# A routed three-way MLP on one core: the first group's rows in two gathers, its first layer by halves of tokens, and GpSimd's set-up moved around the ordering

## The chip, the core and the metric

The kernel runs on one core of one Trainium2 chip. The metric is the device time of one launch in microseconds, the median of three runs; the kernel before takes 102.68 us (101.89 to 102.86).

## What is computed

`x` is 64 sequences of 64 tokens with 256 features, float32. Each sequence has a condition 0, 1 or 2 that picks one of three small networks ("routes"); the result is added to `x` and layer-normalised.

```python
out_nr = gelu(x @ w1_nr + b1_nr) @ w2_nr + b2_nr                       # condition 0, 256 -> 256 -> 256
out_tsr = gelu(x @ w1_tsr + b1_tsr) @ w2_tsr + b2_tsr                  # condition 1
h = gelu(x @ w1_sr + b1_sr)                                            # condition 2, 256 -> 512
out_sr = gelu(h @ w2_sr + b2_sr) @ w3_sr + b3_sr
out = where(c == 0, out_nr, where(c == 1, out_tsr, where(c == 2, out_sr, 0)))
y = x + out
return (y - mean(y)) * rsqrt(var(y) + 1e-5) * gamma + beta
```

## The kernel before

**Ordering.** The kernel sorts the 64 sequences by route on the chip, so that groups of eight sequences (512 tokens) share one route. GpSimd writes constants (iota, memset, affine_select; L377 to L414) while the conditions are fetched. VectorE (DVE) turns the conditions into one-hot rows `own` (L666), TensorE (PE) counts them (L950, L951), and a chain of small VectorE instructions (L674 to L703) ends in `in_slot` and `row_at`. PE multiplies these (L953) into the row number that each of the 128 partitions has to fetch for each of ten groups, and VectorE converts them to integers, `load_idx` (L711). Each sequence is 16 rows of four tokens (4 KB each), so that eight sequences fill 128 partitions. GpSimd then issues indirect gathers `xs[g] <- x` (L421), the first three at once (`EARLY = 3`).

**Classes and places.** VectorE goes on to the table of the groups' classes (`cls_tab`, L716 to L732), copies the bias columns (L734), makes the low part of the first layer's weights (`w_low(0)`, L742), and builds `at_place` and `half_row_at` (L872 to L887), which PE multiplies into the places for the stores (L1142, L1143) and the rows of a half-size last group (L1146).

**Precision.** Every float32 product is three products of rounded parts. For a tensor `t`, ScalarE (ACT) copies the rounded high part `t_hi` and VectorE subtracts it to get `t_lo`; PE accumulates `w_lo*x_hi + w_hi*x_hi + w_hi*x_lo`. One 128-wide block of the first layer is thus six matmuls (two tiles of the 256 features, `kt`), of 512 columns (tokens) each.

**Steps.** PE transposes a group's rows into the PSUM pair `ps_x` (L962, eight 128x128 transposes), ACT copies `x_hi`, VectorE subtracts `x_lo`, and `layer1` (L979 to L991) runs. For the long route, `long_first` runs four blocks m = 0 to 3 into `ps_a0, ps_a1, ps_b, ps_a0`, ACT applies GELU twice (L563 the rounded part, L564 in place) and VectorE subtracts (`low`, L758). `long_second` is the second layer, `last_layer` (L1024, products L1045) the last. `last_layer` of group g-1 runs in step g. Then VectorE adds x and takes the statistics, GpSimd takes the root and multiplies by gamma and adds beta, and scatters (L480). In this run groups 0 and 1 are long.

**The head of the program.** PE's order is written by hand: ordering matmuls, the bias transpose (L956), ten matmuls on ones that only keep PE busy (`WARM`, L1136), the transposes of group 0 (each half of the features, `kt`, signalled apart), the places, and step 0. In step 0 the transposes of group 1 (`next_x`) stand between block 0 and block 1; ACT's `x_high(1)` and VectorE's `x_low(1)` stand behind their parts of block 0. SP's queue issues the long route's weights, waits for GpSimd's two memsets (`zeroed`, L337), issues the last-layer biases, gamma and beta, waits for group 0's rows (`x_loaded[0]`, L345), and issues the other routes' weights and the broadcast biases. GpSimd's memsets of the unused route's last weights (L428) stand ahead of the first gather. `consts` reaching `CONSTS` (17) says that all GpSimd constants are there; `ORDER_CONSTS` (10) that those of the ordering are.

## Time and profile before

| | |
|---|---|
| median of three runs | 102.68 us (101.89 to 102.86) |
| the profiled execution, its device time | 102.77 us |
| its span, first to last instruction | 101.1 us |
| PE matmul busy | 83.8 us (83%), 502 matmuls |
| PE weight load busy | 73.1 us (72%) |
| VectorE busy | 76.8 us (76%) |
| ScalarE busy | 66.6 us (66%) |
| GpSimd busy | 64.0 us (63%) |
| DMA | 13.01 MB, mean 129 GB/s |

Time that lies outside the span is 102.77 - 101.1 = 1.67 us. Names are PE (TensorE), PEld (its weight loads), DVE (VectorE), ACT (ScalarE), POOL (GpSimd), SP (the queue that issues most direct DMAs). "L962" is a line of the kernel. A matmul's duration includes the time to drain, so the pace of a row of matmuls is read from their starts, not from their durations.

### The profile page before, as it was taken

The page shows a single profiled execution, that of the slowest core. Times are in us where ns is not written, and L with a number is a line of the kernel's source. Part 1 is how long each engine was busy: PE and PEld are TensorE (multiplying, and loading weights), DVE is VectorE, ACT ScalarE, POOL GpSimd, SP SyncE. Part 2 cuts the span into 40 slices and gives each one's busy share as a digit, 9 for nine tenths or more (in the row PEclk, how much of TensorE's full clock was granted, in tenths as well). Part 3 has the DMA queues.
Part 4 walks back from the last instruction along what each step waited for, and adds up shares of the span by engine and source line. Part 5 has one row for each costly group of instructions (what it writes and reads, how often), then busy time and mean ns, then how long its engine had stood idle before and what let it go on. Part 6 is the DMA issues. An engine that isn't in the chain of part 4 may idle for free.

```text
span 101.1 us, 1747 instructions
## 1 busy us (share of the span) xinstructions
PE 83.8 (83%) x502; PEld 73.1 (72%) x502; DVE 76.8 (76%) x209; ACT 66.6 (66%) x108; POOL 64.0 (63%) x81
## 2 busy tenths in 40 slices
PE   0239999999999999999999999999999999960000
PEld 0137588887886988879989899898988999950000
DVE  5578966849775504985799999899999999899900
ACT  0667046999599503599999899998998990800000
POOL 7918605005977760040567898998889989899900
PEclk9999999999999999999999999999999999999755
DMA  0892899810028999300000220402205005051570
GB/s 0 261 358 47 284 336 321 207 17 0 0 47 311 281 366 409 152 0 6 0 0 6 89 122 6 183 5 96 118 0 208 6 0 214 0 182 39 208 242 20
DMA packets 5782, 13.01 MB, mean 129 GB/s; under 512 B 656, under 2 KB 3104, under 8 KB 5760
## 3 DMA queue, kind: packets, MB, share of 16 engines
q0 software_dynamic: 2672, 9.57, 25.8%
q1 hardware_dynamic: 3068, 3.15, 10.3%
q8 instruction: 12, 0.20, 0.9%
q14 instruction: 10, 0.08, 0.3%
q10 hardware_dynamic: 20, 0.01, 0.0%
HBM read 8.53 MB, written 4.46 MB: 129 GB/s over the span
## 4 chain that ended last, share of the span: by engine, by line
PE 57%; DVE 15%; POOL 10%; ACT 5%; DMA 4%; issue 4%; DVEq 0%; POOLq 0%; ACTq 0%
PE ps_f L1045 14%; PE ps_x L962 7%; PE ps_a L985 7%; PE ps_a L990 6%; PE ps_a L986 6%; DMA xs<-x_dram,load_idx 4%; POOL rstd L456 2%; PE ps_b L1130 2%; PE ps_a L1130 2%; PE ps_b L1127 2%; PE ps_b L1126 2%; PE ps_a L1127 2%; PE ps_a L1126 2%; POOL xs L467 2%; POOL xs L472 2%
## 5 line engine op out<-in xcount | busy, mean ns | idle before, releaser
L985 PE MATMUL ps_a<-x_hi,w_lo 128*128 128x512 f32 (+1 forms) x40 | 16.3, 409 | 0.0
L467 POOL TENSOR_TENSOR xs<-xs,gamma_b 128x768 f32<-128x768 f32 (+1 forms) x7 | 12.4, 1778 | 5.3 <-ACT xs L567 5.1
L986 PE MATMUL ps_a<-x_hi,w_hi 128*128 128x512 f32 (+1 forms) x40 | 15.1, 381 | 0.0
L1045 PE MATMUL ps_f<-wf_lo,f_hi 128*128 x60 | 15.1, 283 | 0.0
L1045 PE MATMUL ps_f<-wf_hi,f_hi 128*128 x60 | 15.0, 283 | 0.0
L564 ACT ACTIVATE ps_a<-ps_a,bias_cols 128x512 f32<-128x512 f32 (+1 forms) x22 | 14.3, 648 | 0.0
L563 ACT ACTIVATE f_hi<-ps_a,bias_cols 128x512 fp32r<-128x512 f32 (+1 forms) x16 | 10.6, 665 | 4.8 <-PE ps_a L1130 4.8
L421 POOL DMA_INDIRECT xs<-x_dram,load_idx x10 | 10.4, 1040 | 5.0 <-issue 2.6
L456 POOL TENSOR_TENSOR rstd<-var_eps,half 128x4 f32<-128x4 f32 (+1 forms) x9 | 9.1, 1007 | 6.9 <-DVE var_eps L787 6.7
L472 POOL TENSOR_TENSOR xs<-xs,beta_b 128x768 f32<-128x768 f32 (+1 forms) x7 | 12.4, 1769 | 0.1
L990 PE MATMUL ps_a<-x_lo,w_hi 128*128 128x512 f32 (+1 forms) x40 | 12.1, 384 | 0.0
L766 DVE TENSOR_TENSOR xs<-ps_f,xs 128x1024 f32<-128x1024 f32 x7 | 8.5, 1219 | 4.3 <-remote 3.8
L1045 PEld LDWEIGHTS ps_f<-wf_lo,f_hi 128*128 128x128 f32 x60 | 11.3, 189 | 0.3
L437 POOL TENSOR_TENSOR wf_lo<-wf_raw,wf_hi 128x512 fp32r<-128x512 f32 x3 | 4.9, 1656 | 10.5 <-ACT wf_hi L531 6.3
L1045 PEld LDWEIGHTS ps_f<-wf_hi,f_hi 128*128 128x128 f32 x60 | 11.3, 189 | 0.3
L758 DVE TENSOR_TENSOR f_lo<-ps_a,f_hi 128x512 fp32r<-128x512 f32 (+1 forms) x16 | 9.9, 647 | 1.4 <-ACT ps_a L564 1.4
L567 ACT ACTIVATE xs<-xs,shift,rstd 128x256 f32<-128x256 f32 x20 | 10.6, 602 | 0.0
L480 POOL DMA_INDIRECT out_dram<-xs,store_idx x8 | 8.4, 1052 | 2.7 <-POOL xs L472 1.4
L770 DVE BATCH_NORM_STATS2 stats<-xs 128x6 f32<-128x256 f32 x28 | 9.8, 414 | 0.2
L1045 PE MATMUL ps_f<-wf_hi,f_lo 128*128 x60 | 9.7, 284 | 0.0
L985 PEld LDWEIGHTS ps_a<-x_hi,w_lo 128*128 128x128 f32 x40 | 7.5, 188 | 2.2 <-DVE h_lo L758 0.5
L747 DVE TENSOR_TENSOR x_lo<-ps_x,x_hi 128x1024 fp32r<-128x1024 f32 x7 | 8.5, 1219 | 0.6 <-ACT x_hi L541 0.5
(168 smaller groups left out, 200.6 us busy)
## 6 DMA issues: line engine op xcount, KB each, us to landing
w_raw<-L_cond_w_sr_dram SPq DMA_DIRECT2D x2, 512.0 KB, 4.4
wf_raw<-L_cond_w_sr_dram SPq DMA_DIRECT2D x1, 256.0 KB, 5.1
w_raw<-L_cond_w_tsr_dram SPq DMA_DIRECT2D x1, 256.0 KB, 5.8
w_raw<-L_cond_w_nr_dram SPq DMA_DIRECT2D x1, 256.0 KB, 6.1
wf_raw<-L_cond_w_tsr_dram SPq DMA_DIRECT2D x1, 256.0 KB, 6.2
wf_raw<-L_cond_w_nr_dram SPq DMA_DIRECT2D x1, 256.0 KB, 6.4
xs<-x_dram,load_idx POOLq DMA_INDIRECT x10, 7.3
gamma_b<-L_cond_gamma_dram SPq DMA_DIRECT2D x1, 128.0 KB
```

Of the source, the lines that this page charges most:

```text
L421: nc.gpsimd.indirect_dma_start(out=xs[s][:, :, :].rearrange("p t h -> p (t h)"), out_offset=None, in_=x_rows, in_offset=bass.IndirectOffse ...
L456: nc.gpsimd.tensor_tensor(rstd[:, g, 0:n], var_eps[:, g, 0:n], half[:, 0:n], ALU.pow).then_inc(rstd_step, 1)
L467: nc.gpsimd.tensor_tensor(tiles, tiles, spread(gamma_b, n), ALU.mult).then_inc(gam_pool, 1)
L472: nc.gpsimd.tensor_tensor(tiles, tiles, spread(beta_b, n), ALU.add).then_inc(o_pool, 1)
L563: nc.scalar.activation(hi, bank, ACT.Gelu, bias=bias)
L564: nc.scalar.activation(bank, bank, ACT.Gelu, bias=bias).then_inc(gelu_done, count)
L567: nc.scalar.activation(dst, xs[g][:, t, :], ACT.Identity, bias=shift[:, g, t:t + 1], scale=rstd[:, g, t:t + 1]).then_inc(z_done, 1)
L758: nc.vector.tensor_tensor(lo, bank, hi.bitcast(F32), ALU.subtract).then_inc(low_done, count)
L985: nc.tensor.matmul(dst, w1_lo[:, kt, cols], xh[:, kt, :], start=(kt == 0), stop=False)
L986: nc.tensor.matmul(dst, w1_hi[:, kt, cols], xh[:, kt, :], start=False, stop=False)
L990: mm = nc.tensor.matmul(dst, w1_hi[:, kt, cols], xl[:, kt, :], start=False, stop=(kt == KT - 1))
L1045: return nc.tensor.matmul(ps[:, b, t * H:(t + 1) * H], stationary[:, kt, (2 * b + t) * P:(2 * b + t + 1) * P], weights[:, bass.ds(f_at + k ...
```

## The change

Five edits, all in the part ahead of step 1:

1. The first group's rows come in two gathers. Each still fills 128 partitions, but takes two tokens a row (2 KB) in place of four. Their index `first_idx` has a product of its own, `first_rows_pt`: the matmul of `row_at` with the first column of `in_slot`, run twice so that the sum is twice the row number (in rows of two tokens), with 0 or 1 added on VectorE.
2. The first group is transposed, rounded, subtracted and, for its first block, multiplied by halves of tokens (256 columns) in place of halves of features. PE has the places and the half group's rows ahead of these transposes now, and `w_low(0)` comes behind `half_row_at` on VectorE.
3. The transposes of group 1, with `x_high(1)` and `x_low(1)`, come one block later.
4. GpSimd's `ident` is written only after `own`, and `bias_b` only after `row_at`; `bf_raw` is cleared by VectorE, and the unused route's last weights by ScalarE, between its rounding copies.
5. `WARM` is 7 in place of 10, and the six comparisons that fill `ended` are one.

```diff
-        WARM = 10
+        WARM = 7
...
+        first_rows_pt = ps_x[:, 0, 0:1]
...
+        def first_half(h):
+            return ps_x[:, h, :].rearrange("p (k n) -> p k n", k=KT)
...
-            sp.wait_ge(zeroed, 2)
+            sp.wait_ge(bf_zeroed, 1)
...
-            nc.gpsimd.memset(ident[:, :], 0.0).then_inc(pool_step, 1)
-            pool.wait_ge(pool_step, 2)
-            nc.gpsimd.affine_select(out=ident[:, :], in_=ident[:, :], compare_op=ALU.not_equal, fill=1.0,
-                                    base=0, pattern=[[-1, P]], channel_multiplier=1).then_inc(consts, 1)
-            nc.gpsimd.memset(bf_raw[:, NONE * H:(NONE + 1) * H], 0.0).then_inc(zeroed, 1)
-            nc.gpsimd.memset(bias_b[:, NONE * H:(NONE + 1) * H], 0.0).then_inc(zeroed, 1)
...
+            pool.wait_ge(own_done, 1)
+            nc.gpsimd.memset(ident[:, :], 0.0).then_inc(pool_step, 1)
...
             nc.gpsimd.memset(half[:, :], -0.5).then_inc(pool_step, 1)
+            pool.wait_ge(place_done, 2)
+            nc.gpsimd.memset(bias_b[:, NONE * H:(NONE + 1) * H], 0.0).then_inc(zeroed, 1)
...
-            none = slice(NONE * KT * H, (NONE + 1) * KT * H)
-            for w in (wf_hi, wf_lo):
-                nc.gpsimd.memset(w[:, none].bitcast(F32), 0.0).then_inc(wf_lo_done, 1)
+            for h in range(2):
+                pool.wait_ge(first_idx_done, h + 1)
+                nc.gpsimd.indirect_dma_start(
+                    out=xs[0][:, 2 * h:2 * h + 2, :].rearrange("p t h -> p (t h)"), out_offset=None,
+                    in_=half_x_rows,
+                    in_offset=bass.IndirectOffsetOnAxis(ap=first_idx[:, h:h + 1], axis=0)
+                ).then_inc(first_loaded if h == 0 else x_loaded[0], 16)
             pool.wait_ge(load_idx_done, 1)
-            for s in range(EARLY):
+            for s in range(1, EARLY):
                 gather(s)
...
+            none_zero(wf_hi)
             w_high(0)
+            none_zero(wf_lo)
             w_high(1)
...
-            for kt in range(KT):
-                act.wait_ge(xT_ready, kt + 1)
-                nc.scalar.activation(x_hi[0][:, kt, :], ps_x[:, kt, :], ACT.Copy).then_inc(x_hi_done, 1)
+            for h in range(2):
+                act.wait_ge(xT_ready, h + 1)
+                nc.scalar.activation(x_hi[0][:, :, h * 2 * P:(h + 1) * 2 * P], first_half(h), ACT.Copy
+                                     ).then_inc(x_hi_done, 1)
...
-                        if s == 0 and m == 0:
+                        if s == 0 and m == 1:
                             x_high(1)
...
+            nc.vector.memset(bf_raw[:, NONE * H:(NONE + 1) * H], 0.0).then_inc(bf_zeroed, 1)
             nc.vector.memset(zeros[:, :], 0.0)
...
+            dve.wait_ge(first_rows_ps, 1)
+            for h in range(2):
+                nc.vector.tensor_scalar(first_idx[:, h:h + 1], first_rows_pt, float(2 * NROWS + h),
+                                        float(2 * NROWS - 2 + h), ALU.add, ALU.min).then_inc(first_idx_done, 1)
             dve.wait_ge(rows_ps, 1)
...
-            w_low(0)
...
+            w_low(0)
+            for h in range(2):
+                toks = slice(h * 2 * P, (h + 1) * 2 * P)
+                dve.wait_ge(x_hi_done, h + 1)
+                nc.vector.tensor_tensor(x_lo[0][:, :, toks], first_half(h), x_hi[0][:, :, toks].bitcast(F32),
                                         ALU.subtract).then_inc(x_lo_done, 1)
...
+            nc.tensor.matmul(first_rows_pt, row_at[:, :], in_slot[:, 0:1], start=True, stop=False)
+            nc.tensor.matmul(first_rows_pt, row_at[:, :], in_slot[:, 0:1], start=False, stop=True
+                             ).then_inc(first_rows_ps, 1)
             nc.tensor.matmul(rows_pt, row_at[:, :], in_slot[:, :], start=True, stop=True).then_inc(rows_ps, 1)
...
+            def layer1_halves(cols, bank, count):
+                for h in range(2):
+                    toks = slice(h * 2 * P, (h + 1) * 2 * P)
+                    dst = bank[:, 0, toks]
+                    pe.wait_ge(x_hi_done, h + 1)
+                    for kt in range(KT):
+                        nc.tensor.matmul(dst, w1_lo[:, kt, cols], x_hi[0][:, kt, toks], start=(kt == 0), stop=False)
+                        nc.tensor.matmul(dst, w1_hi[:, kt, cols], x_hi[0][:, kt, toks], start=False, stop=False)
+                    pe.wait_ge(x_lo_done, h + 1)
+                    for kt in range(KT):
+                        mm = nc.tensor.matmul(dst, w1_hi[:, kt, cols], x_lo[0][:, kt, toks], start=False,
+                                              stop=(kt == KT - 1))
                 mm.then_inc(mm_ready, count)
...
-                layer1(l1_cols(SR, 0), g, ps_a[0], 1)
+                if g == 0:
+                    layer1_halves(l1_cols(SR, 0), ps_a[0], 1)
+                else:
+                    layer1(l1_cols(SR, 0), g, ps_a[0], 1)
+                    pe.wait_ge(low_done, HID * (g - 1) + 5)
+                layer1(l1_cols(SR, 1), g, ps_a[1], 1)
                 if g == 0:
                     next_x(0)
```

The order of PE's instructions before, from the ordering's first product of the rows up to the first block's end (`ps_z` holds the places and the half group's rows):

```order
L953 MATMUL ps_b<-in_slot,row_at 128x10
L956 MATMUL ps_a<-ident,bias_rows 128x16
L1136 MATMUL ps_f<-warm_x,ones 128x512 x10
...
L962 MATMUL ps_x<-ident,xs 128x128 x8
L1142 MATMUL ps_z<-at_place,seq_ones 1x84
L1143 MATMUL ps_z<-at_place,seq_ones 1x84
L1146 MATMUL ps_z<-seq_ones,half_row_at 128x1
...
L985 MATMUL ps_a<-x_hi,w_lo 128x512
L986 MATMUL ps_a<-x_hi,w_hi 128x512
L985 MATMUL ps_a<-x_hi,w_lo 128x512
L986 MATMUL ps_a<-x_hi,w_hi 128x512
L990 MATMUL ps_a<-x_lo,w_hi 128x512 x2
```

And after:

```order
L987 MATMUL ps_x<-in_slot,row_at 128x1
L988 MATMUL ps_x<-in_slot,row_at 128x1
L990 MATMUL ps_b<-in_slot,row_at 128x10
L993 MATMUL ps_a<-ident,bias_rows 128x16
L1196 MATMUL ps_f<-warm_x,ones 128x512 x7
...
L1201 MATMUL ps_z<-at_place,seq_ones 1x84
L1202 MATMUL ps_z<-at_place,seq_ones 1x84
L1205 MATMUL ps_z<-seq_ones,half_row_at 128x1
L1008 MATMUL ps_x<-ident,xs 128x128 x8
...
L1040 MATMUL ps_a<-x_hi,w_lo 128x256
L1041 MATMUL ps_a<-x_hi,w_hi 128x256
L1040 MATMUL ps_a<-x_hi,w_lo 128x256
```

Two products of one column (on PE each is two passes, as is L953) now stand ahead of the product for all groups and of the bias transpose, there are three warm matmuls fewer, the three lines into `ps_z` have moved ahead of the transposes, and the first block works on 256 columns at a time.

VectorE before, from the integers for the gathers to the first `x_lo`, the classes left out:

```order
L711 TENSOR_SCALAR load_idx<-ps_b 128x10
L713 TENSOR_SCALAR store_idx<-ps_b 128x10
...
L727 TENSOR_SCALAR ended<-slot_id,ends 1x11 x6
L731 TENSOR_REDUCE cls_f<-ended 1x11
L732 CAST cls_tab<-cls_f 1x11
L734 COPY bias_cols<-ps_a 128x16
L742 TENSOR_TENSOR w_lo<-w_raw,w_hi 128x2x512
L872 SCALAR_TENSOR_TENSOR place<-base,rank 64x1
L874 TENSOR_SCALAR near<-nth 64x1
...
L887 SCALAR_TENSOR_TENSOR half_row_at<-half_row_place,half_place,half_row_val 64x128
L892 TENSOR_TENSOR x_lo<-ps_x,x_hi 128x512 x2
```

And after:

```order
L741 TENSOR_SCALAR first_idx<-ps_x 128x1 x2
L744 TENSOR_SCALAR load_idx<-ps_b 128x10
L746 TENSOR_SCALAR store_idx<-ps_b 128x10
...
L759 TENSOR_TENSOR ended<-slot_id,ends 1x66
L763 TENSOR_REDUCE cls_f<-ended 1x11
L764 CAST cls_tab<-cls_f 1x11
L766 COPY bias_cols<-ps_a 128x16
L903 SCALAR_TENSOR_TENSOR place<-base,rank 64x1
...
L918 SCALAR_TENSOR_TENSOR half_row_at<-half_row_place,half_place,half_row_val 64x128
L774 TENSOR_TENSOR w_lo<-w_raw,w_hi 128x2x512
L925 TENSOR_TENSOR x_lo<-ps_x,x_hi 128x2x256 x2
```

`first_idx` is new and stands first, `ended` is one instruction, and `w_lo` has gone from ahead of `place` to behind `half_row_at`.

GpSimd before, from the last constant to the first gathers:

```order
L412 IOTA half_row_val 64x128
L414 MEMSET half 128x4
L428 MEMSET wf_hi 128x512
L428 MEMSET wf_lo 128x512
L421 DMA xs<-x_dram,load_idx 128x1024 x3
```

And after:

```order
L417 IOTA half_row_val 64x128
L421 MEMSET ident 128x128
L423 AFFINE_SELECT ident<-ident 128x128
L425 MEMSET half 128x4
L427 MEMSET bias_b 128x256
L442 DMA xs<-x_dram,first_idx 128x512 x2
L434 DMA xs<-x_dram,load_idx 128x1024 x2
```

Two large memsets are gone, `ident` and `bias_b` have come here, and the next group's gather is now third in the queue.

## Rows read from the trace of the kernel before

**Rows 1.** Waits of PE: line, releaser: us in total, times, longest.

```profile
PE ps_x L962 <- DMA xs<-x_dram,load_idx: 0.2, 1, 0.2
```

**Rows 2.** Chain that ended last, in order of time: start us, us, what.

```profile
7.75 4.34 DMA xs<-x_dram,load_idx
...
15.38 0.46 PE ps_a L990 x2
...
33.25 2.88 PE ps_f L1045 x24
...
68.08 0.89 PE ps_x L962 x8
```

**Rows 3.** Timeline of PE, 6 to 17 us: start us, us, line, operation.

```profile
6.65 0.59 PE L953 MATMUL ps_b<-in_slot,row_at 64*128 64x10 f32 x2 [2.19 <-DVE row_at L703]
...
7.39 4.63 PE L1136 MATMUL ps_f<-warm_x,ones 128*128 128x512 f32 x10
12.23 1.35 PE L962 MATMUL ps_x<-ident,xs 128*128 128x128 f32 x8 [0.20 <-DMA xs<-x_dram,load_idx]
...
13.88 0.38 PE L1146 MATMUL ps_z<-seq_ones,half_row_at 64*128 64x1 f32 x2
14.19 0.50 PE L985 MATMUL ps_a<-x_hi,w_lo 128*128 128x512 f32 x1
...
15.68 1.04 PE L962 MATMUL ps_x<-ident,xs 128*128 128x128 f32 x8
```

**Rows 4.** Timeline of ACT, 6 to 14 us.

```profile
6.88 1.06 ACT L527 ACTIVATE w_hi<-w_raw 128x1024 fp32r<-128x1024 f32 x1 [0.40 <-DMA w_raw<-L_cond_w_sr_dram]
...
13.18 1.09 ACT L603 ACTIVATE x_hi<-ps_x 128x512 fp32r<-128x512 f32 x2 [3.78 <-PE ps_x L962]
```

**Rows 5.** Timeline of DVE, 3 to 15 us.

```profile
3.28 0.47 DVE L666 TENSOR_SCALAR own<-route_id,key 64x4 f32<-64x4 f32 x1
...
4.96 0.42 DVE L687 TENSOR_SCALAR past_tsr<-over,tsr_far 64x8 f32<-64x8 f32 x1
...
7.28 0.17 DVE L711 TENSOR_SCALAR load_idx<-ps_b 128x10 int32<-128x10 f32 x1 [0.53 <-PE ps_b L953]
...
8.36 0.20 DVE L723 TENSOR_SCALAR kinds<-kinds,cnt 64x1 f32<-64x1 f32 x1
...
8.79 0.89 DVE L727 TENSOR_SCALAR ended<-slot_id,ends 1x11 f32<-1x11 f32 x6
...
10.12 1.20 DVE L742 TENSOR_TENSOR w_lo<-w_raw,w_hi 128x1024 fp32r<-128x1024 f32 x1
11.26 0.14 DVE L872 SCALAR_TENSOR_TENSOR place<-base,rank 64x1 f32<-64x1 f32 x1
...
12.56 0.34 DVE L887 SCALAR_TENSOR_TENSOR half_row_at<-half_row_place,half_place,half_row_val 64x128 f32<-64x128 f32 x1
13.81 1.29 DVE L892 TENSOR_TENSOR x_lo<-ps_x,x_hi 128x512 fp32r<-128x512 f32 x2 [0.91 <-ACT x_hi L603]
```

**Rows 6.** Timeline of POOL, 4 to 12 us.

```profile
4.16 0.24 POOL L412 IOTA half_row_val<- 64x128 f32 x1
...
4.84 0.52 POOL L428 MEMSET wf_lo<- 128x512 f32 x1
...
9.18 0.95 POOL L421 DMA_INDIRECT xs<-x_dram,load_idx  x1 [0.31 <-issue]
```

**Rows 7.** Landing of the second gather (L421), then of the third, each alone.

```profile
DMA to landing us min/median/max: 5.1/5.1/5.1
...
DMA to landing us min/median/max: 7.0/7.0/7.0
```

**Rows 8.** Last-layer weights: landing (page, part 6), issue and next use (timelines).

```profile
wf_raw<-L_cond_w_nr_dram SPq DMA_DIRECT2D x1, 256.0 KB, 6.4
...
13.55 0.47 SPq L349 DMA_DIRECT2D wf_raw<-L_cond_w_nr_dram  x1
...
22.20 1.15 ACT L527 ACTIVATE w_hi<-w_raw 128x512 fp32r<-128x512 f32 x2
```

More of the change, by code:

```diff
@@ L523, in _, with none_zero @@
             nc.scalar.activation(ident_r[:, :], ident[:, :], ACT.Copy).then_inc(ident_done, 1)
+            def none_zero(w):
+                nc.scalar.activation(
+                    w[:, NONE * KT * H:(NONE + 1) * KT * H].rearrange("p (a n) -> p a n", n=P),
+                    ident[:, :].rearrange("p (a n) -> p a n", a=1).broadcast_to([P, KT * H // P, P]),
+                    ACT.Copy, scale=0.0).then_inc(wf_lo_done, 1)
             def w_high(i):
@@ L626, in act_step @@
                              HID * s + SHORT[m], SHORT_STEP[m])
-                        if s == 0 and m == 0:
+                        if s == 0 and m == 1:
                             x_high(1)
@@ L725, in _ @@
             chain(nc.vector.tensor_tensor_scan(ends[:, :], kinds[0:1, :], zeros[:, :], 0.0, ALU.add, ALU.add))
-            for r in range(ROUTES + 2):
-                nc.vector.tensor_scalar(ended[:, :, r], slot_id[0:1, :], ends[:, r:r + 1], None, ALU.is_ge
-                                        ).then_inc(dve_step, 1)
-            step[0] += ROUTES + 2
-            dve.wait_ge(dve_step, step[0])
+            chain(nc.vector.tensor_tensor(
+                ended[:, :, :],
+                slot_id[0:1, :].rearrange("b (s r) -> b s r", r=1).broadcast_to([1, GROUPS, ROUTES + 2]),
+                ends[:, :].rearrange("b (s r) -> b s r", s=1).broadcast_to([1, GROUPS, ROUTES + 2]), ALU.is_ge))
             chain(nc.vector.tensor_reduce(cls_f[:, :], ended[:, :, :], AX.X, ALU.add))
@@ L889, in _ @@
                                            ).then_inc(half_place_done, 1)
-            for kt in range(KT):
-                dve.wait_ge(x_hi_done, kt + 1)
-                nc.vector.tensor_tensor(x_lo[0][:, kt, :], ps_x[:, kt, :], x_hi[0][:, kt, :].bitcast(F32),
+            w_low(0)
[3 more added lines that the diff above has]
+                nc.vector.tensor_tensor(x_lo[0][:, :, toks], first_half(h), x_hi[0][:, :, toks].bitcast(F32),
                                         ALU.subtract).then_inc(x_lo_done, 1)
@@ L925, in dve_step_of @@
                         low(banks[m][:, 0, :], h_hi[:, m, :], h_lo[:, m, :], HID * s + m + 1, 1)
-                        if s == 0 and m == 0:
+                        if s == 0 and m == 1:
                             x_low(1)
@@ L936, in dve_step_of @@
                         low(ps_a[m][:, 0, :], f[:, m, :], f_l[:, m, :], HID * s + SHORT[m], SHORT_STEP[m])
-                        if s == 0 and m == 0:
+                        if s == 0 and m == 1:
                             x_low(1)
@@ L963, in transpose_x, with transpose_first @@
                                                  xs[g][:, t, kt * P:(kt + 1) * P], ident[:, :])
-                    if g == 0 or kt == KT - 1:
-                        mm.then_inc(xT_ready, 1)
+                mm.then_inc(xT_ready, 1)
+            def transpose_first():
+                for h in range(2):
+                    pe.wait_ge(first_loaded if h == 0 else x_loaded[0], 16)
+                    for kt in range(KT):
+                        for t in range(2):
+                            mm = nc.tensor.transpose(first_half(h)[:, kt, t * P:(t + 1) * P],
+                                                     xs[0][:, 2 * h + t, kt * P:(kt + 1) * P], ident[:, :])
+                    mm.then_inc(xT_ready, 1)
             def transpose_half(g):
@@ L987, in layer1 @@
                 for kt in range(KT):
-                    if g == 0:
-                        pe.wait_ge(x_lo_done, kt + 1)
                     mm = nc.tensor.matmul(dst, w1_hi[:, kt, cols], xl[:, kt, :], start=False, stop=(kt == KT - 1))
+                mm.then_inc(mm_ready, count)
+            def layer1_halves(cols, bank, count):
+                for h in range(2):
+                    toks = slice(h * 2 * P, (h + 1) * 2 * P)
[5 more added lines that the diff above has]
+                    pe.wait_ge(x_lo_done, h + 1)
+                    for kt in range(KT):
+                        mm = nc.tensor.matmul(dst, w1_hi[:, kt, cols], x_lo[0][:, kt, toks], start=False,
+                                              stop=(kt == KT - 1))
                 mm.then_inc(mm_ready, count)
@@ L1019, in short_first @@
                         pe.wait_ge(low_done, HID * (g - 1) + SHORT[m])
-                    layer1(l1_cols(route, m), g, ps_a[m], SHORT_STEP[m])
                     if g == 0 and m == 0:
-                        next_x(0)
+                        layer1_halves(l1_cols(route, m), ps_a[m], SHORT_STEP[m])
+                    else:
+                        layer1(l1_cols(route, m), g, ps_a[m], SHORT_STEP[m])
+                if g == 0:
+                    next_x(0)
             def last_layer(g):
```

17 lines of the change are left out of this document (10 added, 7 removed).

## The prediction

> **What bounds the kernel now.** I read the waits of PE first. Behind its ordering products PE waited once, 0.2 us for the first rows [rows 1]; from then on its matmuls follow each other without a gap the profile would name. The chain that ended last says the same: DMA of the first rows from 7.75 for 4.34 us, then PE from 12.2 to about 69 us [rows 2], and from there ACT, VectorE and GpSimd, which follow PE's groups. So two things matter: when PE's dense stream begins, and whether anything the change makes late breaks it. All edits lie in the head, so I mark one place, the start of the transposes of group 1 at 15.68, when block 0 is done [rows 3], and work out how far it moves. Behind it PE has the same work, only in another order, so the end should move by as much.
>
> Then I read the head by engine. First rows landed at 12.09 (7.75 + 4.34), transposes start at 12.23, ACT rounds from 13.18 [rows 4], VectorE subtracts 13.81 to 15.10 [rows 5], but PE could not begin block 0 before 14.19, behind the places and L1146 [rows 3]. From there it needs six matmuls.
>
> **Part by part.**
>
> *The ordering.* `own` took 0.47 us and `past_tsr` 0.42 while GpSimd wrote constants (its memset of `wf_lo` runs to 5.36) [rows 5, 6]; the like of them with GpSimd idle, L723, took 0.20. In the new order the constants ahead of `own` end about 1.1 us earlier than 4.40 [rows 6], so `own` runs alone. Savings between 0 (they are slow for another reason) and 0.27 + 0.22; `past_tsr` lies half beside its neighbour, so I take 0.4.
>
> *Row products.* The one-column product is four passes where L953 was two. From L953 to the first warm matmul, two passes and a small transpose took 0.74 [rows 3], so 0.25 a pass. At L1146 (same stationary shape, later) a pass took 0.15 (13.88 to 14.19, two passes). PE is in the same slow stretch as L953, so I take 0.25. The first index comes 2 x 0.25 later, `load_idx` and all behind it on VectorE 4 x 0.25 later. Two indices of 0.17 lie within that wait.
>
> *First gathers.* The first index is ready 0.5 - 0.4 = 0.1 later than `load_idx` was; issues go out at 7.85 and, one slot of 1.43 later (9.18 - 7.75), at 9.28 [rows 2, 6]. The second gather before landed at 9.18 + 5.1 = 14.28, 2.2 us behind the first [rows 7]: 512 KB cost 2.2 us when the queue is full, so 256 KB cost 1.1. A half then lands 4.34 - 1.1 = 3.24 after issue: 11.1 and 12.52. The other bound is that a half takes as long as a whole, 4.34: 12.2 and 13.62. I take the short ones, since back to back the queue was bound by bytes.
>
> *VectorE.* `half_row_at` ended at 12.90. It moves by -0.4 (ordering), +1.0 (passes), -0.74 (six comparisons of 0.89 become one of 0.15) and -1.14 (`w_low(0)` goes behind it, 10.12 to 11.26) [rows 5]: 11.62. `w_low(0)` then ends at 12.8, ahead of its first use.
>
> *PE.* Warm matmuls begin at 7.39 - 0.4 + 1.0 = 8.0 and, at 0.43 each (4.63 for ten, with drain), end at 11.0: in nobody's way. L1146 takes 0.31 behind `half_row_at`, and now stands ahead of the transposes: they start at 11.62 + 0.05 + 0.31 = 11.98, 0.25 earlier than before. The place for a gain was the arrival of the rows, but the transposes wait for the places instead.
>
> *Block 0.* All shifts by 0.25: ACT rounds half 0 at 12.93 to 13.48 and half 1 to 14.02 (0.55 each) [rows 4]; half 1's rows, at 12.52, are transposed by 13.3, in time. VectorE subtracts 13.56 to 14.20 and to 14.85 (0.645 each) [rows 5]. A 256-column matmul costs 0.12 (2.88 for 24) against 0.23 (0.46 for two) [rows 2], so block 0 is 12 x 0.12, the same work. PE: 13.53 + 4 x 0.12 = 14.01; low part at 14.25 + 0.24 = 14.49; + 0.48 = 14.97; + 0.24 = 15.21. Against 15.68 that is **0.47 us gained**: 0.25 from the start, 0.22 because PE no longer stands behind L1146 when x is ready.
>
> *Costed at nothing.* ScalarE's two clears, some 0.6 each, fall into idle time: it waited 0.40 ahead of the second weights' rounding and 3.78 ahead of x [rows 4]; without the latter they would cost 0.8. Group 1's gather is one slot later, issued at 10.7; with 5.1 to landing it is there at 15.8, and the transposes want it behind block 1, at 15.21 + 1.4 = 16.6. In the old place (15.2) it would have stalled PE by 0.6: that is what the moved transposes hide. SP's weights go out behind half 1's landing, 0.4 later than before; the last landed at 13.55 + 6.4 = 20.0 and ACT turns to them at 22.2, now 21.7 [rows 8].
>
> Sum: 102.68 - 0.47 = **102.2 us**; against the profiled execution, 102.77 - 0.47 = 102.3. Its time was 0.09 above the median.
>
> **The clock.** Of PE's clock the trace shows this: the page's granted share reads full throughout the head, yet the ten warm matmuls start 0.43 us apart and those of block 0 0.23 [rows 2, 3], the two levels of 1.2 and 2.4 GHz; PE was busy from 6.65 to 12.0 before the faster pace appears. After the change warm-up has three matmuls less and is followed, from 11.0 to about 13.5, by half-empty stretches. If PE is still at the lower level at block 0, it runs 12 x 0.21: 13.53 + 0.84, + 0.42, + 0.84, + 0.42 = 16.05. That is 0.4 later than before, 103.1; each further 512-column matmul at that level adds 0.2, so through block 1 as well it is 1.6, 104.3. The Trainium skill (TensorE: Matmul & The Clock Gate, section Part 1: The HAM clock gate) says that the slow level is the default, that sustained activity releases it, that this is a matter of time and not of a number of matmuls, and that it varies from run to run of one kernel. By that rule the shorter warm-up is a risk and not a saving; the trace agrees in that ten matmuls in a row stayed slow.
>
> **The rivals.**
>
> *A (0.20): PE's clock stays low into block 0 or 1.* As priced, 103.1, up to 104.3. For it: less warm-up, and it is followed by gaps. Against it: PE is busy from 6.2 to 11.0 with little pause, and three missing matmuls are 1.3 us. It decides from the point where block 0 itself is slow.
>
> *B (0.16): rows late.* If a half lands as late as a whole, 13.62, the last low part is ready at 13.62 + 0.14 + 0.95 + 0.63 + 0.64 = 15.98 and block 0 ends at 16.27, 0.6 later than before: 103.3. It decides from a landing of 13.0. Its sister is group 1's rows: with the third gather's 7.0 in place of 5.1 [rows 7] they land at 17.7 and PE waits 1.1, also about 103.3. For it: 128 descriptors, whatever their size. Against it: the gap of 2.2 between whole gathers.
>
> *C (0.20): the ordering gains more.* With passes of 0.15 and 0.5 off the chain, half rows come 0.5 earlier: 101.7; with GpSimd's share in the other small operations perhaps 101.5. For it: `own` at 0.47 against 0.20. Against it: most of the chain ran with an idle GpSimd already.
>
> *D, nothing changes (within the forecast's 0.3)* is part of my own case: at 0.1 saved in the ordering the gain is 0.2.
>
> **How the numbers follow.** Forecast 0.44: 101.8 to 102.6. A measurement of this kernel can tell about 1% (1.03 us) from no change. Faster by more needs a gain twice mine: C nearly whole, 0.20. Slower by more than 1% (above 103.7) is the longer half of A, and B with both parts, 0.14. The rest, 0.66, is within 1%. The range runs from C to B and the shorter half of A: 101.4 to 103.4.
>
> **What would show it.** `own` near 0.2 and the first gather issued within 0.2 of 7.75: the ordering's term. `half_row_at` ending near 11.6 and the first transposes right behind L1205 and not behind a DMA: the new limit. Second half landed before 13. Block 0's 256-column matmuls 0.12 apart (0.21: rival A). Start of group 1's transposes with no DMA wait, 1.4 us behind block 0. And all of it kept at the end: the chain from there as before. I am wrong if block 0 ends outside 14.7 to 15.6.

## The result, and the profile after

The changed kernel takes 105.29 us (median of six, 104.43 to 106.24) against 102.28 us for the kernel before (six runs, 101.83 to 103.04). The ratio is 1.025, 95% interval 1.0202 to 1.0299: it is slower, where I had forecast 0.5 us faster and a range that ended at 103.4. The profiled execution took 104.67 us with a span of 103.0, so it is one of the quicker ones; the span is 1.9 us above that of the kernel before. Here and below a ratio leaves out executions more than 1.5% above the fastest of the same kernel, and since the clock makes just such differences, median and range stand beside it.

The waits of PE behind the ordering, all of them:

```profile
PE ps_z L1201 <- DVE at_place L916: 1.1, 1, 1.1
PE ps_a L1040 <- ACT x_hi L630: 0.3, 1, 0.3
```

The one wait for the first rows [rows 1] is gone. Two others have come: 1.1 us ahead of the places, and 0.3 us ahead of block 0. The timeline of PE (start us, us, operation), which answers to [rows 3]:

```profile
7.79 3.35 PE L1196 MATMUL ps_f<-warm_x,ones 128*128 128x512 f32 x7
12.21 0.30 PE L1201 MATMUL ps_z<-at_place,seq_ones 64*1 64x84 f32 x2 [1.07 <-DVE at_place L916]
...
12.90 1.09 PE L1008 MATMUL ps_x<-ident,xs 128*128 128x128 f32 x8
14.34 0.47 PE L1040 MATMUL ps_a<-x_hi,w_lo 128*128 128x256 f32 x1 [0.34 <-ACT x_hi L630]
14.61 0.41 PE L1041 MATMUL ps_a<-x_hi,w_hi 128*128 128x256 f32 x1
14.82 0.41 PE L1040 MATMUL ps_a<-x_hi,w_lo 128*128 128x256 f32 x1
...
16.95 0.63 PE L1028 MATMUL ps_a<-x_hi,w_lo 128*128 128x512 f32 x1
...
18.76 1.03 PE L999 MATMUL ps_x<-ident,xs 128*128 128x128 f32 x8
```

The warm-up ends at 11.1, PE then does nothing until 12.21. Block 0 starts 0.15 later than before, but its matmuls of 256 columns start 0.21 us apart and not 0.12, so that it ends at 16.95 and not at 15.68. Block 1 takes 1.81 where 1.40 is its price. The stretches of the same trace (stretch, length, PE busy, granted clock, DMA share, GB/s) say why:

```profile
11.00:12.00 1.00, 0.14 (x1) 1.00 0.66 176
...
13.00:14.00 1.00, 0.99 (x8) 1.00 0.84 279
14.00:15.00 1.00, 0.67 (x3) 0.71 0.56 212
15.00:16.00 1.00, 1.00 (x7) 0.50 0.68 185
16.00:17.00 1.00, 1.00 (x7) 0.50 0.72 249
17.00:18.00 1.00, 1.00 (x4) 0.58 1.00 347
18.00:19.00 1.00, 1.00 (x7) 1.00 1.04 336
```

The granted clock falls to half at about 14.4 us and is back a little before 18. It had been at the upper level by 12.21: the two products for the places and the transposes run at the faster pace. In the kernel before it never fell until the products were over, at 94.7. The other engines, in the rows that answer to [rows 5, 6]; the last line is SP's first issue behind the landing of the second half:

```profile
3.29 0.22 DVE L695 TENSOR_SCALAR own<-route_id,key 64x4 f32<-64x4 f32 x1
...
4.71 0.22 DVE L716 TENSOR_SCALAR past_tsr<-over,tsr_far 64x8 f32<-64x8 f32 x1
...
7.24 0.22 DVE L741 TENSOR_SCALAR first_idx<-ps_x 128x1 int32<-128x1 f32 x2 [0.94 <-PE ps_x L988]
...
11.07 0.34 DVE L918 SCALAR_TENSOR_TENSOR half_row_at<-half_row_place,half_place,half_row_val 64x128 f32<-64x128 f32 x1
```

```profile
7.70 1.14 POOL L442 DMA_INDIRECT xs<-x_dram,first_idx  x1 [1.19 <-DVE first_idx L741]
9.15 0.97 POOL L442 DMA_INDIRECT xs<-x_dram,first_idx  x1 [0.31 <-issue]
...
DMA to landing us min/median/max: 3.6/3.7/3.7
...
12.88 0.38 SPq L358 DMA_DIRECT2D w_raw<-L_cond_w_tsr_dram  x1
```

`own` and `past_tsr` fell to 0.22, the halves landed at 11.4 and 12.8. Behind the head all is as before: the last transposes on the chain start at 69.73 against 68.08 [rows 2], 1.65 later.

```profile
69.73 0.89 PE ps_x L999 x8
```

Of the 1.9 us between the two spans, then, 1.7 are there when group 2 is transposed, the first mark behind the head at which both kernels have done the same work (28.08 against 26.35). VectorE's last rows come 1.5 later (96.79 against 95.28), and so does the first issue of the last stores (97.99 against 96.49). From there to the end of the span it is 4.6 us before and 5.0 after. In the sixteen traces of this document that stretch, the same code in all, lies between 4.6 and 5.8, so these 0.4 are scatter.

### The profile page after: what moved, and what is told of

It is laid out like the page before. It is cut to its first block, busy times and chain, and to the rows that moved or that the text cites. A ratio compares the mean times of both kernels' runs of the same rounds, so it can differ in the third digit from the quotient of the medians.

```text
span 103.0 us, 1757 instructions
## 1 busy us (share of the span) xinstructions
PE 84.6 (82%) x509; PEld 74.4 (72%) x509; DVE 76.5 (74%) x207; ACT 67.5 (66%) x110; POOL 63.8 (62%) x79
## 3 DMA queue, kind: packets, MB, share of 16 engines
q1 hardware_dynamic: 3068, 3.15, 9.7%
## 4 chain that ended last, share of the span: by engine, by line
PE 58%; DVE 17%; POOL 9%; ACT 5%; issue 5%; DVEq 0%; POOLq 0%; ACTq 0%
PE ps_f L1105 14%; PE ps_a L1028 6%; PE ps_a L1029 6%; PE ps_x L999 6%; PE ps_a L1031 6%; POOL rstd L474 2%; PE ps_b L1187 2%; PE ps_b L1186 2%; PE ps_a L1187 2%; PE ps_a L1186 2%; PE ps_a L1190 2%; PE ps_b L1190 2%; POOL xs L485 2%; POOL xs L490 2%; DVE ps_x L846 2%
## 5 line engine op out<-in xcount | busy, mean ns | idle before, releaser
L1028 PE MATMUL ps_a<-x_hi,w_lo 128*128 128x512 f32 (+1 forms) x38 | 15.5, 412 | 0.0
L1031 PE MATMUL ps_a<-x_lo,w_hi 128*128 128x512 f32 (+1 forms) x38 | 11.5, 383 | 0.0
L434 POOL DMA_INDIRECT xs<-x_dram,load_idx x9 | 9.2, 1023 | 2.6 <-issue 2.4
```

The lines of the kernel that those rows point to most:

```text
L1028: nc.tensor.matmul(dst, w1_lo[:, kt, cols], xh[:, kt, :], start=(kt == 0), stop=False)
L1031: mm = nc.tensor.matmul(dst, w1_hi[:, kt, cols], xl[:, kt, :], start=False, stop=(kt == KT - 1))
```

## The experiments

Ratios are to the kernel before, timed beside it on the same chip, with the 95% interval. Three chips were used, so two ratios are compared more loosely than each is known: a_warm10, b_warm7, a_noload and b_setup share one, the four kernels that are kept busy another, and the rest a third.

**Ten warm matmuls in the changed kernel (a_warm10).**

```diff
-        WARM = 7
+        WARM = 10
```

> The changed kernel with ten warm matmuls in place of seven, nothing else. Theory W (the shorter warm-up, with the idle stretch behind it, let PE's clock fall at 14.3 us, and blocks 0 and 1 ran at the lower level): the granted clock stays 1.00 from 12 to 20 us, the 256-column matmuls stand 0.12 apart, block 0 ends near 15.8 in place of 16.95, and the kernel takes about 103.0 us, 1.6 less than the changed kernel in its profiled run. Rival H (the pauses of the work by halves let it fall whatever the warm-up): the clock still falls near 14 us and the time stays at 104.5 or more.

103.46 us (102.62 to 105.06, ten runs), ratio 1.0057 (1.0021 to 1.0092). Most of the loss is gone: 1.025 has become 1.006. Its profile happens to be of its slowest execution, 105.06, and shows another way to lose the same time:

```profile
7.80 4.63 PE L1196 MATMUL ps_f<-warm_x,ones 128*128 128x512 f32 x10
...
13.53 1.97 PE L1008 MATMUL ps_x<-ident,xs 128*128 128x128 f32 x8
...
15.77 0.42 PE L1041 MATMUL ps_a<-x_hi,w_hi 128*128 128x256 f32 x1
...
17.05 0.28 PE L1041 MATMUL ps_a<-x_hi,w_hi 128*128 128x256 f32 x1
17.16 0.28 PE L1040 MATMUL ps_a<-x_hi,w_lo 128*128 128x256 f32 x1
```

Here the transposes took 1.97 in place of 1.09 and the matmuls stood 0.21 apart until 16.8, then 0.12: the clock had not risen in time, and block 0 ended at 17.63 and not near 15.8 as expected. The page's granted share reads 1.00 through all of this, as it does during the warm-up; ahead of its first change that column does not show the lower level, and the pace of the matmuls has to be read.

**Seven warm matmuls in the kernel before (b_warm7).**

```diff
-        WARM = 10
+        WARM = 7
```

> The kernel before with seven warm matmuls in place of ten, nothing else. Theory W: warm-up ends at 10.6, PE then idles until the first rows at 12.1, the clock falls near 14 us and blocks 0 and 1 run at the lower level: 1.2 to 1.8 us slower, about 104. Rival H: no difference from the kernel before, since its transposes and block 0 follow each other closely.

Four runs: 104.92, 106.36, 106.73 and 102.82; median 105.64 against 102.83. With four runs so far apart I give no ratio. The stretches of the trace, of the first of them:

```profile
11.00:12.00 1.00, 0.00 (x0) 1.00 0.82 258
...
14.00:15.00 1.00, 1.00 (x4) 0.55 0.73 280
...
16.00:17.00 1.00, 1.00 (x5) 0.50 0.76 195
17.00:18.00 1.00, 1.00 (x8) 0.74 1.00 352
```

One constant makes a loss as large as the whole change (2.8 us by the medians, against 3.0) and the same fall of the clock, with no halves and no other edit. The pauses of the work by halves are not needed to explain the fall.

The fall is only one way to lose, though. Every execution has a mean granted clock on record. Where a trace shows the fall in the head it is 0.949 to 0.953; in the traces without, 0.954 to 0.969. The fall alone, 3.4 us at half, takes 0.017 off the mean, and the end of the run, low in every trace behind the last product, 0.030 or more; a mean above 0.96 has no room for both. Of the six executions of the changed kernel two have 0.951 and 0.947 (104.67 and 105.48 us); the other four (104.43, 105.10, 105.76 and 106.24) have 0.963 to 0.970, so no such stretch was recorded in them. The two slowest of b_warm7, 106.36 and 106.73, have 0.967 and 0.963. They lost in some other way, and since the granted share does not show a clock that has not yet risen, the late rise of a_warm10's profile fits; a_noload, below, shows it with seven warm matmuls.

**Ten, but three of them early (b_early3).** Of ten warm matmuls in the kernel before, three stand behind the counts, where PE is idle.

```diff
-        WARM = 10
+        WARM = 7
+        EARLY_WARM, POST_WARM = 3, 0
...
+            def keep_warm(n):
+                for i in range(n):
+                    nc.tensor.matmul(ps_f[:, i % 2, :], ones2[:, :], warm_x[:, :], start=True, stop=True)
+
+            keep_warm(EARLY_WARM)
             pe.wait_ge(place_done, 2)
```

> The kernel before with ten warm matmuls, three of which stand behind the counts (4.4 to 5.9 us, where PE has nothing to do) and seven in the old place; so as many as before, but they end at 10.6 and PE idles until the rows at 12.1. If it is the idle stretch ahead of group 0 that costs the clock: like the kernel before with seven, most runs at 104.5 to 106.5. If it is the number of warm matmuls (total activity of the head) that counts: like the kernel before, 102 to 103.4.

104.66 us (103.89 to 105.61, six runs) against 103.06 us, ratio 1.0158 (1.0089 to 1.0226). PE:

```profile
4.34 1.65 PE L955 MATMUL ps_f<-warm_x,ones 128*128 128x512 f32 x3
...
7.36 3.36 PE L1142 MATMUL ps_f<-warm_x,ones 128*128 128x512 f32 x7
12.21 1.07 PE L968 MATMUL ps_x<-ident,xs 128*128 128x128 f32 x8 [1.49 <-DMA xs<-x_dram,load_idx]
```

As many matmuls, the same idle stretch of 1.5 us ahead of group 0, and a little over half of the loss: 1.6 us by the medians, against 2.8 with seven. Its clock stood at 0.50 from 15 to 17 us. The three executions with the fall (mean clock 0.951 to 0.953) took 103.89 to 104.26, the three without (0.968 to 0.972) 105.05 to 105.61. So the number of warm matmuls does not save it; where they stand counts. What this run doesn't part is the idle stretch from the length of the unbroken row, seven in place of ten. The run bs_gather, below, bears on that. Its PE idles 1.0 us behind ten in a row that end at 12.0, about as long as in the changed kernel (1.1 us behind seven that end at 11.1), and its clock, at the upper level within the row, does not fall; its six runs lie within 0.4 us.

**PE kept busy through the head (b_keep, a_keep, bs_keep, a_keep_noload).** Four warm matmuls early, nine in the old place, six behind the wait for the bias columns, in four kernels: before, changed, before with the set-up edits (below), and changed with PE's classes as constants. The edit of b_keep:

```diff
-        WARM = 10
+        WARM = 9
+        EARLY_WARM, POST_WARM = 4, 6
...
+            keep_warm(EARLY_WARM)
             pe.wait_ge(place_done, 2)
...
             pe.wait_ge(bias_done, 1)
+            keep_warm(POST_WARM)
             pe.wait_ge(tab_done, 1)
```

> The kernel before with PE kept busy through the head: four warm matmuls behind the counts, nine in place of ten behind the bias transpose, six more behind the wait for the bias columns. Theory W (most of the spread of the head comes from where PE's clock rises or falls): the clock is at the upper level from about 11 us on in every run, transposes 0.11 apart, and the runs lie at the lower edge of the kernel before, 101.8 to 102.3, with less spread than its 102.0 to 103.4. Rival: the clock had risen in time anyway and the extra matmuls delay the transposes: 0.1 to 0.5 slower.

> The changed kernel with the same filling. Theory W: no stretch below 1.00 of granted clock, 256-column matmuls 0.12 apart, block 0 ends near 15.8, the runs at 102.3 to 102.9, 2.3 us or more below the changed kernel. What is then left against the same filling of the kernel before (0.1 to 0.4) is the cost of the new structure alone. Rival H (halves let the clock fall): still a stretch at 0.50 near 14 to 17 us and a time above 104.

> The kernel before with the set-up edits and the same filling. If the set-up edits are worth 0.4 in the order, and PE's first block does not wait for other things: 0.3 to 0.4 below the filled kernel before, near 101.6. If block 0 waits behind the places in both (the places' table on VectorE is ready no earlier), under 0.1.

> The changed kernel with the same filling, PE's class registers set to constants instead of loaded. Theory L: places begin at 11.4 or 11.5 rather than 12.2, and block 0 ends 0.6 to 0.8 earlier than in the filled changed kernel, the time 0.6 to 0.8 less. Rival: the second half's rows, landed at 12.8, are the next limit, and the gain is 0.2 or less.

b_keep: 103.82 us, ratio 1.0036 (0.9957 to 1.0116). a_keep: 104.71, 1.0138 (1.0076 to 1.0201). bs_keep: 103.34, 1.0004 (0.9938 to 1.0071). a_keep_noload: 104.55, 1.0131 (1.006 to 1.0203). Four runs each. My expectation for the times was wrong in all four. In b_keep PE was busy from 3.9 us on, with one pause of 0.2, and the clock still rose only at about 13.2, where it rose at about 12.8 in the kernel before. In the other three it rose at 11.2 to 11.8, but the matmuls that were put in stood in the way by then. In b_keep the last of them ran at the slow pace and pushed the transposes to 13.68 (first fence); in a_keep the places began at 13.27 (second).

```profile
11.38 2.46 PE L955 MATMUL ps_f<-warm_x,ones 128*128 128x512 f32 x6
13.68 1.03 PE L968 MATMUL ps_x<-ident,xs 128*128 128x128 f32 x8
14.65 0.30 PE L1149 MATMUL ps_z<-at_place,seq_ones 64*1 64x84 f32 x2
...
16.83 1.03 PE L968 MATMUL ps_x<-ident,xs 128*128 128x128 f32 x8
```

```profile
13.27 0.30 PE L1208 MATMUL ps_z<-at_place,seq_ones 64*1 64x84 f32 x2
...
13.96 1.09 PE L1014 MATMUL ps_x<-ident,xs 128*128 128x128 f32 x8
15.39 0.35 PE L1046 MATMUL ps_a<-x_hi,w_lo 128*128 128x256 f32 x1 [0.34 <-ACT x_hi L631]
...
17.07 0.39 PE L1034 MATMUL ps_a<-x_hi,w_lo 128*128 128x512 f32 x1
```

What they do show is the structure at the upper level of the clock, which all four had at block 0. The work to compare is the transposes, the places and block 0, in whichever order. The kernel before takes 3.15 us for it (13.68 to 16.83), the changed one 3.80 (13.27 to 17.07). In the old order the places and `half_row_at`'s product, 0.68 us from 14.65 on, fill the time in which ACT and VectorE make x ready; in the new one they stand ahead of the transposes, and PE waits 0.34 for `x_hi` instead. From the first transpose alone the halves reach the end of block 0 in 3.1 us, no sooner than the old order does with the places in between. So at the upper level the new structure costs PE 0.65 us. With the filling in the way, a_keep_noload says nothing on the class load.

**PE's classes as constants (a_noload).** The classes of this input are written into PE's registers instead of loaded.

```diff
-            cls = load_classes(pe, "pe_cls")
+            cls_regs = [pe.alloc_register(f"pe_cls{s}") for s in range(GROUPS)]
+            for r, c in zip(cls_regs, (1, 1, 2, 2, 2, 3, 3, 3, 4, 6, 6)):
+                pe.reg_mov(r, c)
```

> The changed kernel, but PE sets its eleven class registers to the constants of this input and does not load them from the table that VectorE wrote; everything else is computed as before. In the changed kernel the places were ready for PE at 11.4 and began at 12.2. Theory L (the load behind bias_done costs PE about 2 us, 10.1 to 12.2): the places begin at 11.4 and the first half's transposes at 12.0, block 0 starts 0.8 earlier, and the time falls by 0.8 if the clock falls all the same; if with less idle time the clock holds, by 2.4. Rival: PE waited for something else (the places' semaphores or its own queue), and nothing moves.

103.88 us (101.9 to 104.9, ten runs), ratio 0.9972 (0.9928 to 1.0017). The places began 0.57 earlier than 12.21, though the clock was low in this execution:

```profile
11.64 0.43 PE L1204 MATMUL ps_z<-at_place,seq_ones 64*1 64x84 f32 x2 [0.47 <-DVE at_place L916]
...
15.47 0.41 PE L1041 MATMUL ps_a<-x_hi,w_hi 128*128 128x256 f32 x1
...
16.06 0.28 PE L1040 MATMUL ps_a<-x_hi,w_lo 128*128 128x256 f32 x1
16.18 0.28 PE L1041 MATMUL ps_a<-x_hi,w_hi 128*128 128x256 f32 x1
```

`at_place` ended at about 11.4 in both. So in the changed kernel PE was held by its class load. It can't start before the table and the bias columns are ready, at 10.1, and is over at 12.2; that it fills all of these 2.1 us is not shown. The clock here did not fall: it had not risen before about 15.9, where the 256-column matmuls go from 0.21 to 0.12 apart, and the granted share reads 1.00 all along. Four of the ten runs lie at 101.9 to 102.8, six at 103.8 to 104.9, so with seven warm matmuls and a shorter idle stretch (0.47) the head is sometimes quick. The time carries both effects and I don't split it.

**The set-up edits alone (b_setup).** The kernel before with edit 4 and the single comparison; no halves, one gather, ten warm matmuls.

```diff
+            pool.wait_ge(own_done, 1)
+            nc.gpsimd.memset(ident[:, :], 0.0).then_inc(pool_step, 1)
...
-            for r in range(ROUTES + 2):
-                nc.vector.tensor_scalar(ended[:, :, r], slot_id[0:1, :], ends[:, r:r + 1], None, ALU.is_ge
-                                        ).then_inc(dve_step, 1)
...
+            chain(nc.vector.tensor_tensor(
+                ended[:, :, :],
...
+            none_zero(wf_hi)
             w_high(0)
+            none_zero(wf_lo)
             w_high(1)
```

> The kernel before with the set-up edits alone: GpSimd's ident, bias_b and clears moved or given to the other engines, and one comparison for ended. No halves, ten warm matmuls. Set-up theory: own takes 0.22 as in the changed kernel, row_at ends 0.45 earlier, the first gather is issued 0.45 earlier, and block 0 starts 0.4 earlier: about 0.4 us faster than before. Rival: transposes wait for something else than the rows (PE's class load behind bias_done), and the gain is under 0.2.

102.14 us (101.77 to 103.02, ten runs), ratio 0.9939 (0.9902 to 0.9976): faster by 0.6%. GpSimd's and PE's rows:

```profile
7.33 1.13 POOL L424 DMA_INDIRECT xs<-x_dram,load_idx  x1 [0.79 <-DVE load_idx L720]
```

```profile
11.83 1.72 PE L970 MATMUL ps_x<-ident,xs 128*128 128x128 f32 x8
```

The gather goes out 0.42 earlier than at 7.75 and the transposes start 0.40 earlier than at 12.23. This part of the change does what my sum said. In the profiled execution, the slowest of the ten, the transposes ran slow (1.72) and took the gain back.

**Two gathers, but whole-group work (bs_gather).** The set-up edits and the split gather with its own row product; the transposes wait for both halves.

```diff
+            nc.tensor.matmul(first_rows_pt, row_at[:, :], in_slot[:, 0:1], start=True, stop=False)
...
+            pe.wait_ge(first_loaded, 16)
             transpose_x(0)
```

> The kernel before with the set-up edits and the first rows in two gathers with their own row product, but transposed, rounded and multiplied as a whole group behind both. The last of group 0's rows should land at 12.8 as in the changed kernel, against 11.7 with one gather (set-up edits alone), so the transposes start 1.0 later: about 0.9 us slower than the set-up edits alone, 0.3% above the kernel before. If the clock also reacts (idle time behind the warm-up), more: 1.5 or above. Rival: the transfers are so overlapped that both halves are there by 12.0, and nothing is lost.

103.64 us (103.36 to 103.76, six runs), ratio 1.0103 (1.0064 to 1.0142). PE waited 1.0 us for the rows; the ten warm matmuls took 4.21 and not 4.63, so the clock rose within them:

```profile
7.82 4.21 PE L1163 MATMUL ps_f<-warm_x,ones 128*128 128x512 f32 x10
13.03 1.07 PE L989 MATMUL ps_x<-ident,xs 128*128 128x128 f32 x8 [1.01 <-DMA xs<-x_dram,first_idx]
```

Against 11.8 with one gather the whole group is there 1.2 later: 0.39 for the extra passes of the row product (first issue 7.72 against 7.33) and the rest for the second issue's slot of 1.45, less what a smaller transfer saves. Set beside b_setup (on another chip), the split gather with its row product costs about 1.6% where nothing uses the early half.

**Places ahead of the transposes (bs_places), group 1 a block later (bs_nextx), the old order in the changed kernel (a10_order).** The first two are the set-up edits and one edit more (bs_places also has `w_low(0)` behind `half_row_at`; bs_nextx moves the work of ACT, shown, and of VectorE and PE), the third is a_warm10 with its transposes ahead of the places.

```diff
-            transpose_x(0)
             pe.wait_ge(at_place_done, 2)
...
+            transpose_x(0)
```

```diff
-                        if s == 0 and m == 0:
+                        if s == 0 and m == 1:
                             x_high(1)
```

```diff
+            transpose_first()
             pe.wait_ge(at_place_done, 2)
...
-            transpose_first()
```

> The kernel before with the set-up edits, and PE's places and half-group rows ahead of group 0's transposes (with w_low(0) behind half_row_at on VectorE, as in the changed kernel). One gather, whole group, ten warm matmuls. Theory P (in the changed kernel the transposes stand behind the places, and this is what keeps it 0.6 above the kernel before even with ten warm matmuls): transposes start 0.7 later than 11.8, block 0 starts 0.3 or more later than with the set-up edits alone, and the kernel is 0.3 to 0.5 slower than those (102.14 on another chip, 0.6% under the kernel before). Rival: PE has these 0.7 us of work to do ahead of block 0 in either order, and nothing changes: 0.6% under the kernel before.

> The kernel before with the set-up edits and group 1's transposes, x_high and x_low one block later. Every engine has the same work, and the long second layer's waits have 0.5 us to spare: no change against the set-up edits alone (0.6% under the kernel before). Rival: ACT and VectorE reach the later blocks too late and PE idles: 0.3 us or more slower.

> The changed kernel with ten warm matmuls and the old order of PE around group 0: transposes ahead of the places. Theory P: the first half's transposes start at 12.2 in place of 12.9, block 0's start is then set by the second half's rows or by the places behind it, and the time is 0.3 to 0.6 below that of the changed kernel with ten warm matmuls (1.0057 of the kernel before), so about equal to the kernel before. Rival: the second half's rows, landed at 12.8, and the products by halves set the end of block 0, and nothing moves: 1.004 to 1.008.

bs_places: 102.85 us (101.48 to 104.58), ratio 0.9973 (0.9931 to 1.0015). bs_nextx: 102.57 (101.85 to 103.32), 0.9999 (0.996 to 1.0038). a10_order: 102.96 (102.3 to 103.39), 1.0024 (0.9994 to 1.0054). Twelve runs each; the ratio of bs_places is that of its seven quicker ones, and its median is 0.2% above the kernel before. None differs clearly from its neighbour: 0.9973 and 0.9999 beside 0.9939 for the set-up edits, and 1.0024 beside 1.0057, with intervals that overlap, and on another chip. The later transposes of group 1 cost nothing in the traces: block 0 ends 0.82 earlier in bs_nextx than in b_setup (14.84 against 15.66), since its clock rose sooner, and group 2 is transposed 0.83 earlier. By the ratios the order of the places is worth some 0.3%, which these runs can't tell from nothing. Its effect on PE is plain in the third: the transposes start at 12.24, right behind the warm-up, and block 0 at 14.43, behind the places:

```profile
12.24 1.57 PE L1008 MATMUL ps_x<-ident,xs 128*128 128x128 f32 x8
...
14.43 0.39 PE L1040 MATMUL ps_a<-x_hi,w_lo 128*128 128x256 f32 x1
...
15.96 0.39 PE L1028 MATMUL ps_a<-x_hi,w_lo 128*128 128x512 f32 x1
```

The same work as above takes 3.72 us here (12.24 to 15.96), with transposes that ran 0.5 long because the clock was still low: about 3.2 at the upper level, an estimate from these rows, and not 3.80. By it the order of the places, and not the halves, costs most of the 0.65; the times, 0.3% apart, can't confirm it.

**Twelve warm matmuls on the set-up edits (bs_warm12).**

```diff
-        WARM = 10
+        WARM = 12
```

> The kernel before with the set-up edits and twelve warm matmuls. They end at 12.3 where the clock is still low, 0.5 behind the rows. If longer activity makes a late rise of the clock rarer: the upper end of the spread shrinks and the median stays at that of the set-up edits (0.994 of the kernel before) or falls below. If ten are already enough there: 0.2 to 0.5 us slower than with ten, since the transposes start later.

101.71 us (101.64 to 102.32, six runs) against 103.06 us, ratio 0.9891 (0.9841 to 0.9942). It beats the kernel before, which the changed one doesn't. How much of this is the two more matmuls and how much the set-up edits (0.9939 alone, on another chip) is not parted. PE:

```profile
7.13 4.48 PE L1144 MATMUL ps_f<-warm_x,ones 128*128 128x512 f32 x12
11.52 1.09 PE L970 MATMUL ps_x<-ident,xs 128*128 128x128 f32 x8
...
14.73 1.03 PE L970 MATMUL ps_x<-ident,xs 128*128 128x128 f32 x8
```

Twelve took less time than ten in the kernel before [rows 3], so the clock rose within them, and they end as the rows land. Group 1's transposes start at 14.73, 0.95 earlier than at 15.68.

## Why the prediction was wrong

*The ordering.* Right: `own` and `past_tsr` fell to 0.22 and the counts came earlier; the set-up edits moved the first gather by 0.42, where I had 0.4.

*Row products and gathers.* Nearly right. First issue 7.70 (7.85 forecast), second 9.15 (9.28). A half takes 3.6 to 3.7 to land, not 3.24, against 4.34 for a whole: the term "512 KB cost 2.2 us when the queue is full, so 256 KB cost 1.1" was too kind by 0.4, and the second half came at 12.8, not 12.52, still short of the 13.0 from which rival B decides. Group 1's rows landed with no wait.

*VectorE.* `half_row_at` ended at 11.41, forecast 11.62.

*PE's start.* Wrong by 0.9: transposes at 12.90, forecast 11.98. The sentence "L1146 takes 0.31 behind `half_row_at`, and now stands ahead of the transposes" left out two things that stand ahead of both. One is PE's load of the class registers, which held the places until 12.21 though `at_place` had ended at 11.4; a_noload shows 0.57 of it. That it ended unseen in the kernel before, where PE's start at 12.23 stands right behind the landing of the rows, is likely and not shown. The other is the two products for the places themselves, 0.38 (12.21 to 12.59).

*The warm-up.* This is the step that failed and that makes the result: that the warm matmuls "end at 11.0: in nobody's way". I costed three removed matmuls at nothing because they were off the path. Taking them out of the kernel before costs 2.8 us (b_warm7), and putting them back into the changed one leaves 0.6 of its 3.0 (a_warm10). I did price rival A, but at a chance of 0.20, with "PE is busy from 6.2 to 11.0 with little pause" as the evidence against; b_early3, busy from 3.9 on with pauses, still lost 1.6. For the block, the price was right: 12 x 0.21 = 2.5 for block 0, where 14.34 to 16.95 is 2.6, and block 1 was low only in part, 1.81. For the kernel it was low: 103.1, up to 104.3, where the median is 105.29. And the mechanism was only half mine. I had the clock staying low into block 0. In the profiled execution it was up by 12.21 and fell again at 14.4; in the four executions without that fall a clock that stays low fits, as said. What I missed most is that such executions are the rule with seven and not one in five.

The Trainium skill (TensorE: Matmul & The Clock Gate, section HAM oscillation — how this bites in real kernels) describes a clock that falls back behind a wait for data; the waits it tells of are longer than these. This trace shows such a fall behind less: 1.1 us of idle ahead of the places and 0.34 ahead of block 0, then a granted clock of 0.50.

*Block 0 by halves.* A loss of 0.65 at the upper level (3.80 against 3.15 us for transposes, places and block 0). My 0.22 from "PE no longer stands behind L1146" was not saved: the same matmuls now stand ahead of the transposes, where they fill no waiting time. With ten warm matmuls the rest of the change is 0.6% slower than before, while the set-up edits in it are 0.6% faster. These 0.65 are the shown part of that difference, with the 0.39 by which the extra passes of the row product put off what stands behind them. The later landing of the last rows is not: they were there at 12.8, PE waited for no DMA, and its transposes started at 12.90.

**What stays open.** The median difference is 3.0 us, and the one profiled execution of the changed kernel lost 1.9. Of the five others four lost more, and four have no recorded fall; the late rise seen in the profiles of a_warm10 and a_noload would do it, but no trace of the changed kernel itself shows it. What decides between the two is open too, as is how much of the loss goes with the idle stretch and how much with the shorter row.

## What to carry to other kernels

Matmuls that do nothing are on the path if they are what keeps PE busy up to the first real work. Before shortening a warm-up, look at the idle time it leaves ahead of the first dense stretch, time the kernel ten times and not three, and read the pace of equal matmuls in that stretch. Splitting a transfer to start on its first half pays only if the last half does not come later than the whole did and if PE has nothing else queued ahead: here the second issue slot (1.45 us) outweighed the smaller transfer (0.7 us). Small products that fill a wait should stay in it: moved ahead of the transposes, they cost 0.65 us here. And a wait that ends with a DMA may hide a second one, such as a register load, that ends just before.

## What the runs showed of the hardware that I had not expected

- PE busy from 3.9 us on, in b_keep, did not raise the clock before about 13.2 us, later than without the early matmuls (12.8, the kernel before); once it rose within the warm-up, between 10 and 11 us (bs_warm12), once only at 16.8, nine microseconds into unbroken work (a_warm10).
- An idle stretch of 1.1 to 1.5 us ahead of group 0 was followed, some 2 us later and with PE at work again, by 3 to 3.5 us at the lower level, in three kernels with seven warm matmuls in a row. Behind ten in a row an idle stretch of 1.0 us was not (bs_gather).
- PE's load of eleven class registers lies between 10.1, when the table is ready, and the next matmul at 12.2; at least 0.57 us of it held PE.
- VectorE's small operations with a per-partition scalar took 0.42 to 0.47 us beside GpSimd's memsets and 0.22 without. The second `at_place` (64 x 4) took 0.42 in the changed kernel, while GpSimd issued a gather, and 0.22 in the kernel before, with GpSimd idle.
